# Block transposes on VectorE with round trips through DRAM instead of transposes on TensorE, and an order that spans two batches

## The reference

```python
x = x + _layernorm(_L0_attn_ref(_layernorm(x), Wq, Wk, Wv, Wo))
x = x + _layernorm(_L0_ffn_ref(_layernorm(x), W, b, logits, u))
# attention: q, k, v = x@Wq, x@Wk, x@Wv; scores = q k^T, masked above the diagonal;
#            softmax(scores / 16) v @ Wo
# ffn: idx = argmax(log_softmax(logits) - log(-log(u))); x @ W[idx] + b[idx]
```

## Time and profile before

| | before |
|---|---|
| device time, median of 3 runs | 425.56 us (425.23 to 426.36) |
| profiled execution, first to last instruction (span) | 424.3 us |
| busy: PE, DVE, ACT, POOL | 414.0, 339.8, 299.1, 118.3 us |
| busy share of the span: PE, DVE, ACT, POOL | 98%, 80%, 71%, 28% |
| granted TensorE clock, mean | 0.997 |
| bytes moved by the DMA queues | 18.46 MB, 13.5% of the 16 engines' span |

### The profile page before, as it was taken

The page is one execution under the profiler, slowest core; times in us unless marked ns, Lnnn a source line. Parts: engine busy times, 40 slices in busy tenths (PEclk is TensorE's granted clock), DMA queues, the critical chain, the costliest instruction groups (busy, mean ns, idle before and its releaser), DMA issues.

```text
span 424.3 us, 9812 instructions
## 1 busy us (share of the span) xinstructions
PE 414.0 (98%) x3045; PEld 393.2 (93%) x3045; DVE 339.8 (80%) x1010; ACT 299.1 (71%) x854; POOL 118.3 (28%) x237
## 2 busy tenths in 40 slices
PE   7999999999999999999999999999999999999993
PEld 7789999999999999999999999999999999999993
DVE  4578778987898878887788878898788887876776
ACT  5886877668766687568866687666885678756563
POOL 3103333232322232123421323223232224302133
PEclk9999999999999999999999999999999999999998
DMA  6310012110120101201021001201012000020003
GB/s 198 90 49 26 26 25 76 52 39 14 51 81 18 49 25 42 82 9 40 25 66 57 25 25 48 76 25 49 13 37 99 0 0 0 25 75 2 2 0 101
DMA packets 18951, 18.46 MB, mean 44 GB/s; under 512 B 1140, under 2 KB 18932, under 8 KB 18932
## 3 DMA queue, kind: packets, MB, share of 16 engines
q1 hardware_dynamic: 18660, 17.96, 13.5%
q10 hardware_dynamic: 272, 0.26, 0.2%
HBM read 9.83 MB, written 8.39 MB: 43 GB/s over the span
## 4 chain that ended last, share of the span: by engine, by line
PE 93%; DMA 2%; ACT 2%; DVE 1%; issue 0%; POOL 0%; SPq 0%; POOLq 0%; DVEq 0%
PE bank L805 54%; PE score L805 23%; PE bank L908 7%; PE bank L932 3%; PE bank L819 3%; DMA wq<-in_L_attn_Wq_dram 1%; DMA bias_raw<-in_L_ffn_b_dram 1%; PE score L891 1%; PE score L847 0%; PE bank L865 0%; POOL f_rstd L387 0%; PE score L835 0%; DVE out_sb L778 0%; ACT squares_junk L591 0%; ACT sums_junk L470 0%
## 5 line engine op out<-in xcount | busy, mean ns | idle before, releaser
L387 POOL TENSOR_TENSOR o_rstd<-o_ve,minus_half 128x1 f32<-128x1 f32 x64 | 35.2, 550 | 193.8 <-DVE o_ve L735 193.8
L805 PE MATMUL bank<-v_hi,pT_lo 128*128 128x256 f32 x288 | 84.6, 294 | 0.0
L805 PE MATMUL bank<-v_hi,pT_hi 128*128 128x256 f32 x288 | 81.4, 283 | 0.0
L805 PE MATMUL bank<-v_lo,pT_hi 128*128 128x256 f32 x288 | 81.3, 282 | 0.0
L805 PE MATMUL score<-xT_hi,g_lo 128*128 128x384 f32 (+4 forms) x176 | 63.7, 362 | 0.0
L805 PE MATMUL score<-xT_hi,g_hi 128*128 128x384 f32 (+4 forms) x176 | 61.1, 347 | 0.0
L805 PE MATMUL score<-xT_lo,g_hi 128*128 128x384 f32 (+4 forms) x176 | 61.1, 347 | 0.0
L549 ACT ACTIVATE probs<-neg_scores,neg_max 128x128 f32<-128x128 f32 (+3 forms) x64 | 49.7, 776 | 14.0 <-DVE neg_max L707 13.5
L805 PEld LDWEIGHTS bank<-v_lo,pT_hi 128*128 128x128 f32 x288 | 55.0, 191 | 0.4
L805 PEld LDWEIGHTS bank<-v_hi,pT_lo 128*128 128x128 f32 x288 | 54.9, 191 | 0.3
L805 PEld LDWEIGHTS bank<-v_hi,pT_hi 128*128 128x128 f32 x288 | 54.9, 191 | 0.0
(11 more groups left out here) (112 smaller groups left out, 1130.5 us busy)
## 6 DMA issues: line engine op xcount, KB each, us to landing
x_sb<-in_L_attn_x_dram SPq DMA_DIRECT2D x32, 256.0 KB, 2.7
out_dram<-out_sb SPq DMA_DIRECT2D x31, 256.0 KB, 2.1
wq<-in_L_attn_Wq_dram ACTq DMA_DIRECT2D x1, 256.0 KB, 4.1
wk<-in_L_attn_Wk_dram SPq DMA_DIRECT2D x1, 256.0 KB, 4.4
wv<-in_L_attn_Wv_dram SPq DMA_DIRECT2D x1, 256.0 KB, 4.2
wo_raw<-in_L_attn_Wo_dram SPq DMA_DIRECT2D x1, 256.0 KB, 4.5
wf_raw<-in_L_ffn_W_dram SPq DMA_DIRECT2D x1, 256.0 KB, 2.7
out_dram<-out_sb SPq DMA_DIRECT2D x2, 128.0 KB, 2.1
```

Of the source, the lines that this page charges most:

```text
L387: return nc.gpsimd.tensor_tensor(dst[:, n0:n1], ve[:, n0:n1], minus_half[:, n0:n1], ALU.pow)
L805: last = nc.tensor.matmul(dst, l, r, start=(i == 0), stop=(i == len(passes) - 1))
```

## The change

Most transposes leave PE. For probabilities, xn and y, a step on DVE now transposes the 32 x 32 blocks of a tile from SBUF to SBUF (Q for probabilities, B for xn, I for y). That leaves the blocks in the wrong partitions. The blocks are written to a DRAM tensor (SP's P, W, Y), and each of four fetches (SP's Q, R, J) brings the blocks for 32 partitions back. Then ACT rounds them to the hi halves from SBUF (ACT's P, X, J). POOL subtracts for the lo halves of probabilities and y (POOL's P, J); DVE does it for x (X). In the last batch tiles 4 to 7 and units 1 to 4 are still turned by PE (T, Y), and so is x of the first batch.

The layer now takes y itself, not yn: its weights are centred a second time, along the other direction, by a product with a matrix of 1/256 in batch 0, and 1/std comes in with the bias, on DVE (F). ACT's K is gone. The output is written into f_sb.

The lists now span two batches: a step with a prime belongs to the batch before. PE's O6, O7 and F0 to F3 of a batch come in between the scores of the next. SP has a list of its own.

Blank lines are left out of the diff.

```diff
-    DVE_ORDER = """M0 M1 L0 V0 M2 T0 V1 L1 T1 C0 M3 R0 V2 L2 T2 M4 C1 V3 T3 R1 N0 M5 C2 C3 R2 R3 N1 M6 T4 T5 M7
-        X0 Y0 C4 R4 T6 C5 L3 R5 T7 C6 N2 R6 X1 Y1 C7 F0 R7 N3 G0 Y2 F1 U0 X2 Z0 X3 F2 U1 Y3 U2 Z1 G1
-        F3 Z2 U3 G2 G3 Z3"""
...
+    PE_ORDER = """S0 O6' S1 O7' S2 V0 S3 F0' S4 S5 V1 O0 F1' S6 O1 S7 O2 O3 V2 F2' F3' V3 O4 O5 G0 G1 G2 G3"""
+    ACT_ORDER = """G3' J1' E0 O6' H0 E1 O7' H1 H2 E2 J2' V0 E3 F0' P0 P1 E4 E5 V1 O0 H3 J3' O1 E6 P2 F1' P3 E7 O2 O3 V2 P4
+        P5 F2' F3' X0 V3 X1 O4 X2 O5 X3 J0 G0 G1 P6 P7 G2"""
+    DVE_ORDER = """M0 G2' G3' Q0 L0 L1 L2 C6' M1 R6' B0 Q1 B1 C7' M2 R7' B2 Q2 V0 M3 I3' F0' Q3 N3' M4 U0' M5 L3 Q4 Q5 V1
+        C0 Z0' B3 M6 F1' R0 C1 Q6 R1 M7 U1' I0 N0 Q7 Z1' C2 C3 R2 V2 F2' R3 I1 F3' U2' N1 U3' Z2' X0 X1
+        V3 C4 X2 Z3' X3 R4 C5 G0 R5 I2 G1 N2"""
+    POOL_ORDER = """P7' J1' L0 C6' L1 N2' L2 C7' J2' N3' P0 P1 U0' L3 C0 J3' C1 P2 P3 U1' N0 C2 C3 P4 P5 U2' U3' N1 C4 J0 C5
+        P6"""
+    SP_ORDER = """J2' P0 Q0 Y3' A3' P1 J3' Q1 P2 Z0' W0 Q2 R0 Y0 P3 A0 Z1' J0 Y1 Q3 A1 J1 Z2' Z3' Y2 A2"""
...
+    DVE_LAST = """G2' M0 G3' Q0 F0' M1 U0' Q1 Z0' C6' M2 R6' M3 Q2 F1' Q3 M4 U1' Z1' V0 C7' M5 R7' I3' N3' V1 C0 C1 R0 M6
+        V2 R1 I0 C2 N0 R2 C3 T4 R3 N1 M7 F2' Y1 F3' U2' T5 Z2' V3 U3' C4 Z3' R4 T6 C5 F0 R5 N2 U0 T7 Z0
+        C6 Y2 R6 N3 C7 F1 R7 Y3 N4 F2 F3 U1 Y4 U2 Z1 F4 U3 Z2 U4 Z3 Z4"""
...
+    x_kept = nc.dram_tensor("x_kept", (PART, QUADS, RUN), f32, kind="Internal").ap()
+    y_kept = nc.dram_tensor("y_kept", (NP, PART, QUADS, KC * 2 * QUAD), f32, kind="Internal").ap()
+    p_kept = [nc.dram_tensor(f"p_kept{p}", (PART, QUADS, (4 * p + 3) * QUAD), f32, kind="Internal").ap()
+              for p in range(NP)]
...
+        x_turn = sb("x_turn", [PART, QUADS * RUN])
+        y_turn = sb("y_turn", [PART, NP, QUADS * KC * 2 * QUAD])
+        p_turn = sb("p_turn", [PART, NP * (2 * NP + 1) * PART])
...
+            def fetch(raw, kept, loaded):
+                for q, source in enumerate(kept):
+                    sp.dma_start(raw[q * QUAD:(q + 1) * QUAD].rearrange("a (i r) -> a i r", i=QUADS), source
+                                 ).then_inc(loaded, 16)
...
+                    elif kind == "W":
+                        sp.wait_ge(x_turned, b.count(NP, 0))
+                        sp.dma_start(x_kept.rearrange("p q r -> p (q r)"), x_turn[:, :]).then_inc(x_written, 16)
+                    elif kind == "R":
+                        sp.wait_ge(x_written, b.count(16, 0))
+                        fetch(x_turn[:, :], x_kept.rearrange("(i a) q r -> q a i r", i=QUADS), x_raw_loaded)
+                    elif kind == "P":
+                        sp.wait_ge(p_turned, b.count(NT, 2 * n + 2))
+                        sp.dma_start(p_kept[n].rearrange("p q r -> p (q r)"), p_slot(n)).then_inc(p_written[n], 16)
+                    elif kind == "Q":
+                        sp.wait_ge(p_written[n], b.count(16, 16))
+                        fetch(p_slot(n), p_kept[n].rearrange("(i a) q r -> q a i r", i=QUADS), p_loaded[n])
+                    elif kind == "Y":
+                        sp.wait_ge(y_turned, b.count(NP, n + 1))
+                        sp.dma_start(y_kept[n].rearrange("p q r -> p (q r)"), y_turn[:, n]).then_inc(y_written[n], 16)
+                    elif kind == "J":
+                        sp.wait_ge(y_written[n], b.count(16, 16))
+                        fetch(y_turn[:, n], y_kept[n].rearrange("(i a) q r -> q a i r", i=QUADS), y_loaded[n])
+                    elif kind == "Z":
+                        store(b, n)
...
+                    elif kind == "P":
+                        pool.wait_ge(p_hi_ready, b.count(NT, n + 1))
+                        nc.gpsimd.tensor_tensor(p_half(pT_lo, n), p_quads(n), p_half(pT_hi, n).bitcast(f32),
+                                                ALU.subtract).then_inc(p_lo_ready, 1)
+                    elif kind == "J":
+                        pool.wait_ge(y_hi_ready, b.count(NP, n + 1))
+                        nc.gpsimd.tensor_tensor(y_half(yT_lo, n), y_quads(n), y_half(yT_hi, n).bitcast(f32),
+                                                ALU.subtract).then_inc(y_lo_ready, 1)
...
                     if kind == "E":
...
+                        act.wait_ge(max_ready, b.count(NT, n + 1))
+                        if b.last and n - 2 in LAST_T:
+                            job = Job(b, "T", n - 2, len(t_groups(n - 2)) - 1)
+                            act.wait_ge(bank_full[job.bank], job.used + 1)
+                        elif b.known != 0 or n >= 2:
+                            act.wait_ge(p_turned, b.count(NT, n - 1))
...
+                    elif kind == "P":
+                        act.wait_ge(p_loaded[n // 2], b.count(QUADS * 16, QUADS * 16))
+                        used = Job(b, "O", n - PS) if n >= PS else Job(b.other(-1), "O", n + NT - PS)
+                        act.wait_ge(bank_full[used.bank], used.used + 1)
+                        nc.scalar.activation(p_half(pT_hi, n), p_quads(n), ACT.Identity).then_inc(p_hi_ready, 1)
...
+                    elif kind == "J":
+                        act.wait_ge(y_loaded[n], b.count(QUADS * 16, QUADS * 16))
+                        used = Job(b, "F", n - YS) if n >= YS else Job(b.other(-1), "F", n if n + YS >= NP else n + YS)
+                        act.wait_ge(bank_full[used.bank], used.used + 1)
+                        nc.scalar.activation(y_half(yT_hi, n), y_quads(n), ACT.Identity).then_inc(y_hi_ready, 1)
...
                     elif kind == "X":
-                        x_hi(at("X", n), n)
+                        c, k = n // KC, n % KC
+                        if n == 0:
+                            act.wait_ge(x_raw_loaded, b.count(QUADS * 16, 0))
+                            act.wait_ge(scores_ready, b.count(NT, 0))
+                            for j in range(KC):
+                                nc.scalar.activation(xT_first[:, j, :].rearrange("p (i s) -> p i s", i=QUADS),
+                                                     raw_block(0, j)[:, 0], ACT.Identity)
+                        nc.scalar.activation(split_block(xT_hi, c, k), raw_block(c, k),
+                                             ACT.Identity).then_inc(x_hi_ready, 1)
...
+            def x_blocks(b, p):
+                dve.wait_ge(xn_ready, b.count(NP, p + 1))
+                if b.known != 1 and p == 0:
+                    dve.wait_ge(x_lo_ready, b.count(2 * KC, -2 * KC))
+                turned = x_turn[:, :].rearrange("p (q k t s) -> p t k q s", q=QUADS, k=KC, t=NT)
+                for t in (2 * p, 2 * p + 1):
+                    last = nc.vector.transpose(turned[:, t], xn[:, t, :].rearrange("p (k q a) -> p k q a", k=KC, q=QUADS))
+                last.then_inc(x_turned, 1)
...
+                    elif kind == "Q":
+                        dve.wait_ge(probs_ready, b.count(NT, n + 1))
+                        if b.known != 0:
+                            dve.wait_ge(p_lo_ready, b.count(NT, n + 1 - NT))
+                        nc.vector.transpose(p_quads(n), probs[:, n % 2, 0:(n + 1) * PART].rearrange(
+                            "p (u q a) -> p u q a", q=QUADS, a=QUAD)).then_inc(p_turned, 1)
...
                     elif kind == "X":
-                        x_lo(at("X", n), n)
+                        dve.wait_ge(x_hi_ready, b.count(2 * KC, n + 1 - 2 * KC))
+                        c, k = n // KC, n % KC
+                        nc.vector.tensor_tensor(split_block(xT_lo, c, k), raw_block(c, k),
+                                                split_block(xT_hi, c, k).bitcast(f32), ALU.subtract
+                                                ).then_inc(x_lo_ready, 1)
...
+                        job = Job(b, "O", n)
+                        if b.known != 0 and n % 2 == 0:
+                            dve.wait_ge(out_ready, b.count(NP, n // 2 + 1 - NP))
...
+                    elif kind == "I":
+                        wait_for_y(b, t0, t1)
+                        if b.known != 0:
+                            dve.wait_ge(y_lo_ready, b.count(NP, n + 1 - NP))
+                        turned = y_turn[:, p].rearrange("p (q k t s) -> p t k q s", q=QUADS, k=KC, t=2)
+                        for t in range(t0, t1):
+                            last = nc.vector.transpose(turned[:, t % 2], y[:, t, :].rearrange("p (k q a) -> p k q a",
+                                                                                              k=KC, q=QUADS))
+                        last.then_inc(y_turned, 1)
...
                     elif kind == "F":
...
+                        if b.known != 0:
+                            dve.wait_ge(out_sent[p], b.count(16, 0))
                         dve.wait_ge(bank_full[job.bank], job.used + 1)
-                        nc.vector.tensor_tensor(f_sb[:, p, here, :],
-                                                cols(job.bank, (t1 - t0) * D).rearrange("p (t d) -> p t d", t=t1 - t0),
```

(27 more changed lines are left out.)

533 lines of the change are left out of this document (313 added, 220 removed).

## The result

The changed kernel takes 438.31 us (median of 4, 436.39 to 439.48), the kernel before on the same chip 425.77: ratio 1.0272, 95% interval 1.0225 to 1.0319. It is slower by 2.7%, where I had forecast 2.6% faster. The profiled execution has a span of 437.3 us, 24.2 above my 413.1.

A forecast was written before the change was run, and what follows sets the result against it. The prediction took a ring through the last fetch and G2', period 48.3 us, as the bound: 23.5 + 39 + 289.8 + 60.8 = 413.1 us profiled span, 414.4 for the median, range 408 to 421.

The forecast's parts named there:

- The unit prices: Costs per instruction: DVE block transpose of 1024 columns 1.15 us, POOL subtraction 2.3 ns an element, PE transpose 0.11 us.
- The last batch: Final batch on PE: 51.4 us less 14 transposes (1.5) plus carried-in O6', O7' and four F' (10.9), 60.8 us.
- where I had 42.4: PE's work per middle batch: 68 transposes at 0.11 us leave, so 49.9 falls to 42.4 us.
- The fetch rate: Four DMAs into 32 partitions each: taken as 240 GB/s, between 89 and the full queue's 357.
- I add 0.8: Allowance per batch for small waits in DVE's list ahead of Q7: 0.8 us on a period of 47.5.
- the ring's way through G2': Loop G2', Q7, P3, Q3, P6, P7, G2 across DVE, SP and ACT: asks for a period of 47.5 us.
- 48.3: Forecast period of a middle batch in us: 47.5 plus 0.8 for small waits.
- Rival (c): DVE and POOL block each other at X and Z: 3 us a batch, period 49.6, 421 + 1 us; chance 0.10.
- DVE, 45.4: DVE's work per batch: 42.0 less 8.3, plus 0.7 and 11.0 for block transposes, 45.4 us, above PE.
- rival (a): Fetches at 357 GB/s, DVE the bound with 1.6 us of waits: period 47.0, 404 + 1 = 405 us; chance 0.22.
- Batch 0: First batch, without old work: DVE 34.6 us, but trips as long, so 39 us.
- Rival (b): Fetches at half rate, 180 GB/s: period 51.7 + 0.3, 437 + 1 us, slower than before; chance 0.22.

The follow-up runs named there:

- e_order2_notrip: Changed kernel with one-column statistics instructions, no new stores and fetches, and DVE's and POOL's lists reordered around o_rstd: 418.4 us, ratio 0.9805.
- e_order: Changed kernel with G2 ahead of P6 and P7 in ACT's list: 438.7 us, ratio 1.0299.
- e_shortp: Changed kernel with POOL's subtraction for the probabilities cut to 32 columns of each tile: 429.0 us, ratio 1.0054.
- e_split_notrip: Changed kernel with two-column statistics instructions made one-column and without the new stores and fetches: 424.0 us, ratio 0.9945.
- e_notrip_all: Changed kernel without any of the new stores and fetches; ACT rounds blocks once DVE has turned them: 432.2 us, ratio 1.0125.
- e_shortp_notrip: Changed kernel without the new stores and fetches and with POOL's probability subtraction cut to 32 columns: 422.4 us, ratio 0.99.
- e_split: Changed kernel with x_nm, x_ve, y_ve and f_ve each made as two one-column instructions: 437.6 us, ratio 1.0257.

## Why the prediction was wrong, step by step

- **The unit prices held, but for PE's.** A transpose of 1024 takes 1.17 us from start to start (206.55 to 207.72 in DVE's timeline; forecast 1.15). POOL has 2.34 ns an element (2.3). ACT is busy for 32.81 of 51 us (forecast 31.7), POOL 31.28 (29). The last batch is right to 0.3 us.
- **PE.** At full clock e_order2_notrip has 44.54 us in 48.00, 44.4 a batch, where I had 42.4. Of these 1.1 are no work: before each of PE's seven gaps a batch the last product counts with its whole duration, 0.28 us for a 256-wide one, while 0.12 is what it costs. That leaves 43.3, and a transpose is worth (49.9 - 43.3) / 68 = 0.10 us, a little less than the 0.11 read from six of them. It cost nothing while PE was not the bound, but the gain I hoped to have in reserve was smaller by 1 us a batch.
- **The fetch rate** was 220 to 233 GB/s in the middle stretches for my 240. P3's store took 7.7 us to land (7). But of the way from Q7's end to P6 I had missed little, 15.3 us for 14.9; P6 starts 47.7 us behind M0, not 44.9, since Q7 had ended 2.4 late.
- **The step that failed: "I add 0.8", and the ring's way through G2'.** I closed the ring at G2' and let DVE's list run at its own prices up to Q7 at 30, with 0.8 for all small waits. That made 33.4 us from P6 to the next Q7's end; it was 35.4, and Q7 ended at 32.4. The way leads through POOL's passes of P6, P7 and J1', to which the blocked y_ve and x_nm are tied, and on through waits for xn and o_rstd. e_order (no gain without G2's place) and e_shortp (this leg 33.6, the time 9.3 us less by POOL's passes alone) show both halves. 48.3 plus 2.0 for this leg plus 0.4 for the other is 50.7, which is the period of batch 3; batches 4 to 6 take 50.8 to 51.3. The mean, 51.7, comes from batches 1 and 2, with 54.0 and 52.2, where the clock fell soon behind M0 (0.83 in the first 10 us) and in batch 1 the fetch was ready 2 us later; what each of these is worth there was not separated.
- **Rival (c) had the mechanism and not the place.** I bounded the exclusion by X and Z, with two SBUF inputs, and let them meet a pass with chance 0.3. Only 7 of the 92 did, so their means stayed (685 and 479 ns). In six of the seven one engine waited: five passes of J that an X preceded took 1.64 to 1.69 us, the others 1.28 to 1.31, and one Z took 0.68 us for 0.48. The single-input instructions on two columns, which I had not counted, cost 17.0 us over the six middle batches, 2.8 each. The Trainium skill's page "SBUF — State Buffer", section "Who interferes with whom", names instructions with two SBUF inputs and also tensor_scalar, in its 2-port modes; I had used only the first, and the trace agrees with both.
- **DVE, 45.4.** Without blocking its work is 44.6 us a batch (e_split_notrip, the extra instructions in it), so the sum was right. That DVE is then idle for 4.3 us, where my rival (a) had 1.6, would have been a miss as well: without trips and blocking the period was 48.9, not 47.0.
- **Batch 0**, 43.5 for 39, is no matter of trips or blocking: 43.9 us remain without trips (e_notrip_all) and 42.3 without both (e_shortp_notrip). I did not settle it.
- **The clock** stands nowhere in the forecast. PE now has idle stretches. Before 206:208, where the granted clock is 0.54 (near the level of 1.2 GHz), it had waited 1.88 us for pT_lo at 203.55, and its products started 0.21 us apart instead of 0.12. The middle stretches have 0.97 on average, where PE had never waited before and had 1.00; with the waits shortened (e_order2_notrip) it is 1.00 again. Part of PE's gain is given back there, and where the fall comes right behind M0 it lies in the ring, at 1.2 us a fall (e_split).

Rival (b), slower at 438 by a fetch at 180 GB/s, had the time, 438, by luck: the fetch is slower than a load (220 for 357 GB/s), but not as slow as it says, and removing it altogether returns 6.1 of the 12.5 us.

## What to carry to other kernels

When an engine's work is moved to others that each have 10% of slack, sum their waits in line as carefully as their work: here DVE's work was right, and 3.4 us a batch of waits, blocked instructions and falls of the clock made a forecast gain of 11 us into a loss of 12. A ring may close over any engine's in-order list: name every step from the fetch back to the store, here POOL's passes, O6' on PE, squares and xn on ACT and B1 on DVE. Look at single periods beside their mean; those with and without a fall of the clock told here what e_split's 0.7 us hid. Where two limits lie within a few per cent, take both away in one run before a single edit is called worthless.

## What the runs showed of the hardware

- A vector tensor_scalar from SBUF to SBUF waits out a GpSimd subtraction of two SBUF tensors when it has two columns (28 of 28 ended 24 to 31 ns behind the pass, up to 1715 ns for 162) and not when it has one (53 of 53 in 141 to 154 ns).
- A fetch into 32 partitions moves 220 to 233 GB/s with all 16 engines; two queues raise the rate when they write groups 0 and 2 together (288 and 296 for 261, with the neighbours' traffic), not groups 0 and 1 (248 and 268).
- A DMA whose source pattern begins with a dimension of 4 used a quarter of the engines: share 0.27, 100 GB/s.
- PE, never idle in the middle batches of the kernel before, had clock 1.00; in the changed kernels, where it waits for 1.5 to 3 us at a time, it falls now and then to near the 1.2 GHz level, in which 256-wide products start 0.21 us apart instead of 0.12 (204.5 to 207.7 in the changed kernel).
